# First layer of the sparse feed-forward with features on partitions, biases on 128 rows, six idle products a tile

## The reference

```python
# block 1: E=8 experts, F=1024, each token goes to one expert, weighted by its probability
h = jax.nn.gelu(x @ w1 + bb1, approximate=False)     # per expert, (tokens, F)
y = h @ w2 + bb2                                      # (tokens, 256)
# block 5: F=512, silu, each token goes to two experts, y = t + sum_k w_k * expert_k(t)
# block 7: F=256, gelu, each token goes to one expert, unweighted
```

## Time and profile before

| | |
|---|---|
| time, median of 3 runs (lowest, highest) | 2582.37 us (2580.01, 2584.39) |
| the profiled execution's own time | 2593.29 us |
| its span | 2591.3 us |
| mean granted clock of TensorE | 0.92 of full speed |
| PE busy / PEld busy | 2213.3 us (85%) / 1467.9 us (57%) |
| DVE / ACT / POOL busy | 1561.2 us (60%) / 1411.5 us (54%) / 953.2 us (37%) |
| tiles of block 1, from first to last product | about 319 to 483 us of the span |
| tiles of block 5 | about 1985 to 2135 us |
| tiles of block 7 | about 2496 to 2573 us |

### The profile page before, as it was taken

One profiled execution on the slowest core, in us unless ns is written; L12 is line 12 of the kernel. 1 busy time (PEld: TensorE's weight loads), 2 busy tenths in 40 slices (PEclk: granted clock), 3 DMA queues, 4 the chain that ended last, 5 costly groups with the idle time before them and its releaser, 6 DMA issues. The chain is left out here.

```text
span 2591.3 us, 62717 instructions
## 1 busy us (share of the span) xinstructions
PE 2213.3 (85%) x23986; PEld 1467.9 (57%) x23986; DVE 1561.2 (60%) x3640; ACT 1411.5 (54%) x2999; POOL 953.2 (37%) x1066
## 2 busy tenths in 40 slices
PE   5889399599999999968699999999974993899755
PEld 2556255367777777745456666666652541566533
DVE  3667572476566556636767777777756544556463
ACT  3666563365555555425466666666663542566543
POOL 3443222154444444404423333333322632433043
PEclk8999699799999999969899999999986995999978
DMA  6563361300000000010200000000023214333133
GB/s 129 111 116 71 111 216 38 119 20 14 14 14 8 14 14 2 2 33 1 87 14 9 15 14 9 15 14 9 2 85 103 67 56 124 87 79 73 26 114 109
DMA packets 118581, 139.59 MB, mean 54 GB/s; under 512 B 15072, under 2 KB 107184, under 8 KB 118288
## 3 DMA queue, kind: packets, MB, share of 16 engines
q1 hardware_dynamic: 110900, 115.39, 17.3%
q0 software_dynamic: 7392, 20.19, 2.5%
HBM read 93.25 MB, written 17.47 MB: 43 GB/s over the span
## 5 line engine op out<-in xcount | busy, mean ns | idle before, releaser
L952 DVE TENSOR_REDUCE a_mx<-a_pair 112x2 f32<-112x750 f32 x256 | 238.0, 936 | 194.9 <-PE a_pair L1021 194.9
L1260 POOL TENSOR_TENSOR a_kp<-a_kp 125x512 f16<-125x512 f32 x192 | 217.6, 1158 | 259.1 <-ACT a_kp L1351 259.1
L353 POOL TENSOR_SCALAR a_P<-a_P,a_inv 112x375 f32<-112x375 f32 x256 | 148.4, 593 | 378.5 <-DVE a_inv L484 377.4
L890 ACT ACTIVATE a_PT<-a_pair 125x672 f32<-125x672 f32 x256 | 186.2, 730 | 71.1 <-PE a_pair L1033 66.3
L391 ACT ACTIVATE a_P<-a_masked,a_least 112x375 f32<-112x375 f32 x256 | 153.5, 600 | 83.5 <-DVE a_least L479 81.6
L1394 DVE SCALAR_TENSOR_TENSOR a_k<-a_p,a_k 128x375 f16<-128x375 f32 x128 | 69.3, 547 | 138.7 <-ACT a_k L1307 138.7
L1351 ACT CAST a_kp<-a_kp 125x512 f16<-125x512 f32 x192 | 110.4, 617 | 76.4 <-DVE a_kp L1413 76.4
L572 PE MATMUL a_p<-a_kc,a_wk 128*128 128x375 f16 x768 | 147.1, 327 | 4.3 <-POOL a_kc L347 4.3
L1493 PE MATMUL a_p<-a_kc,a_wk 128*128 128x375 f16 x768 | 142.4, 327 | 6.3 <-POOL a_kc L1252 6.3
L586 PE MATMUL a_p<-a_wv,a_kc 128*125 128x512 f16 x576 | 141.9, 383 | 5.2 <-DVE a_v L518 3.6
L479 DVE CUSTOM_DVE_ANT_0 a_masked<-a_s,a_mask_add 112x375 f32<-112x375 f32 x256 | 129.9, 545 | 27.1 <-PE a_s L609 26.1
(11 more groups left out here) (446 smaller groups left out, 5324.1 us busy)
## 6 DMA issues: line engine op xcount, KB each, us to landing
a_kc<-in_ctxT SPq DMA_DIRECT2D x64, 375.0 KB, 4.0
a_k<-a_k_parts SPq DMA_DIRECT2D x192, 93.8 KB
w_stage<-in_L_ffn_W SPq DMA_DIRECT2D x32, 512.0 KB
w_stage<-in_L_ffn_ew SPq DMA_DIRECT2D x16, 512.0 KB, 6.9
w_stage<-expert_rows SPq DMA_DIRECT2D x16, 448.0 KB, 8.0
a_v_in_sb<-in_ctx SPq DMA_DIRECT2D x16, 375.0 KB
a_q<-a_q_parts SPq DMA_DIRECT2D x48, 112.0 KB, 3.6
w_stage<-in_L_ffn_W SPq DMA_DIRECT2D x16, 256.0 KB, 3.9
```

The costliest lines, as they stand in the source:

```text
L353: pool.tensor_scalar(P[:, p % 4, r, :], P[:, p % 4, r, :], inv[:, p % 4, r:r + 1], 1.0, ALU.mult, ALU.mult).then_inc(P_done, 1)
L890: act.activation(PT[:, p % 4, :, :], pair_bank[slot["turned", p]][0:KP, :, 0:KT * S], ACT.Exp).then_inc(exp_done, 1)
L952: dve.tensor_reduce(mx[:, b % 2, 2 * pair:2 * pair + 2], pair_bank[slot["score", p]][0:S, :, 0:SK], AX.X, ALU.max).then_inc(max_done, 1)
L1260: pool.tensor_tensor(kp16[:, LO, j, hf, r, :, :].rearrange("p c m -> p (c m)"), kp[:, n % 4, :], kp16[:, HI, j, hf, r, :, :].rearrange("p ...
```

## The change

hidden swaps the operands: a 128 x 128 piece of w1h is now stationary and x16 (128 columns) moves, so that features come out on partitions. For each 128 features there is one bias product and six products of 128 columns, in place of one and six of up to 512 columns for a whole block. The transposes of the hidden result, their copies and buffers (turn_parts, turn_h, take_high, take_low, hk, t_bank) go; ACT and DVE split the result in SBUF (high_h, low_h) for all three blocks. Block 1 runs output(j-1) in iteration j (LATE = 1), blocks 5 and 7 output(j-2) as before, with a third buffer for h16. There are four hidden banks (HR) for three. The bias operands rows, pick and ones16 are widened to 128 partitions, with zeros in the rows that are new; POOL clears rows during layernorm_phase. Block 7 has six idle products a tile.

```diff
-BUSY_START, BUSY_TILE = 48, 2
+BUSY_START, BUSY_TILE = 48, 6
-        self.pick = m.sb("pick", [2 * E, E, 128], F16)
+        self.pick = m.sb("pick", [128, E, 128], F16)
-        self.rows = m.sb("rows", [2, E, F + D] if self.flat else [2 * E, F + D], F16)
+        self.rows = m.sb("rows", [128, E, F + D] if self.flat else [128, F + D], F16)
+    def clear_rows(self, pool):
+        pool.memset(self.rows[:, :, :] if self.flat else self.rows[:, :], 0.0).then_inc(self.rows_clear, 1)
     def prepare_act(self, act):
         act.wait_ge(self.bias_in, 16)
+        act.wait_ge(self.rows_clear, 1)
-        layernorm_phase(nc, tag + "n", X, XT, ident, xn=xn, fetch=fetch)
+        layernorm_phase(nc, tag + "n", X, XT, ident, xn=xn, fetch=fetch, prepare=w.clear_rows)
-    HR, YR = 3, 3
+    HR, YR = 4, 3
+    LATE = 2 if early else 1
+    HB = LATE + 1
-        h16 = m.sb("h16", [128, 2, 2, F], F16)
+        h16 = m.sb("h16", [128, HB, 2, F], F16)
-        ident16, ones16, warm = m.sb("ident16", [128, 128], F16), m.sb("ones16", [2, 128], F16), m.sb("warm", [128, 1])
+        ident16, ones16, warm = m.sb("ident16", [128, 128], F16), m.sb("ones16", [128, 128], F16), m.sb("warm", [128, 1])
+                def turn_bias(out, e, cols):
+                    if w.flat:
+                        pe.matmul(out, w.rows[:, bass.ds(e, 1), cols].rearrange("z o f -> z (o f)"), ones16[:, :], start=True, stop=False)
+                    else:
+                        pe.matmul(out, w.rows[:, cols], r.pick[:, bass.ds(e, 1), :].rearrange("p o t -> p (o t)"), start=True,
+                                  stop=False)
...
                     for blk in range(NB):
...
-                        add_bias(bank[:, 0:BW], e, cols, start=True, stop=False)
-                        for i, (x, z) in enumerate(PARTS):
-                            for c in range(DC):
-                                mm = pe.matmul(bank[:, 0:BW], x16[:, j % 2, x, c, :],
-                                               w.w1h[:, z, c, bass.ds(e, 1), cols].rearrange("p o f -> p (o f)"),
-                                               start=False, stop=(i, c) == (2, DC - 1))
-                        mm.then_inc(h_done, 1)
                         for f in range(BW // 128):
                             at = blk * BW + f * 128
+                            out = bank[:, f * 128:(f + 1) * 128]
+                            turn_bias(out, e, slice(at, at + 128))
+                            for c in range(DC):
+                                for x, z in ((HI, HI), (LO, HI), (HI, LO)):
+                                    mm = pe.matmul(out, w.w1h[:, z, c, bass.ds(e, 1), at:at + 128].rearrange("p o f -> p (o f)"),
+                                                   x16[:, j % 2, x, c, :], start=False, stop=(c, z) == (DC - 1, LO))
+                        mm.then_inc(h_done, 1)
...
-                for j in range(NT + 2):
+                for j in range(NT + LATE):
...
-                    if 1 <= j < NT + 1:
-                        (turn_parts if early else turn_h)(j - 1)
-                    if j >= 2:
-                        output(j - 2)
+                    if j >= LATE:
+                        output(j - LATE)
...
                 def high_h(j):
-                    if j >= 2:
-                        act.wait_ge(o_done, j - 1)
+                    if j >= HB:
+                        act.wait_ge(o_done, j - HB + 1)
                     for blk in range(NB):
-                        n = j * NB + blk
-                        act.wait_ge(t_done, n + 1)
-                        act.copy(h16[:, j % 2, HI, blk * BW:(blk + 1) * BW], t_bank[n % 2][:, 0:BW]).then_inc(h_hi, 1)
+                        act.wait_ge(h_made, j * NB + blk + 1)
+                        act.copy(h16[:, j % HB, HI, blk * BW:(blk + 1) * BW],
+                                 hs[:, j % 2, blk * BW:(blk + 1) * BW]).then_inc(h_hi, 1)
```

More of the change, by code:

```diff
@@ L2027, in constants @@
                            pattern=[[1, S]], channel_multiplier=-1).then_inc(self.made, 1)
[L2028 removed]
+        pool.affine_select(out=self.pick[0:2 * E, :, :], in_=self.pick[0:2 * E, :, :], compare_op=ALU.not_equal, fill=1.0, base=0,
                            pattern=[[-1, E], [0, 128]], channel_multiplier=1).then_inc(self.blank, 1)
         pool.wait_ge(self.blank, 3)
[L2031 removed]
+        pool.affine_select(out=self.pick[0:2 * E, :, :], in_=self.pick[0:2 * E, :, :], compare_op=ALU.not_equal, fill=1.0, base=-E,
                            pattern=[[-1, E], [0, 128]], channel_multiplier=1).then_inc(self.made, 1)
@@ L2437, in hidden @@
-                        mm.then_inc(h_done, 1)
[L2439 to L2443, removed]
-                        for f in range(FC):
-                            mm = pe.transpose(t_bank[z][:, f * 128:(f + 1) * 128], hk[:, j % 2, z, f * 128:(f + 1) * 128],
-                                              ident16[:, :])
-                        mm.then_inc(t_done, 1)
@@ L2449, in turn_h @@
[L2449 to L2453, removed]
                         for f in range(BW // 128):
                             at = blk * BW + f * 128
-                            mm = pe.transpose(t_bank[(j * NB + blk) % 2][:, f * 128:(f + 1) * 128], hs[:, j % 2, at:at + 128],
-                                              ident[:, :])
-                        mm.then_inc(t_done, 1)
+                            out = bank[:, f * 128:(f + 1) * 128]
@@ L2704, in _ @@
                             w.make_low(dve, n)
-                    if early and j < NT:
-                        low_parts(j)
-                    if 1 <= j < NT + 1:
-                        (take_low if early else low_h)(j - 1)
-                    if j >= 2:
-                        add_y(j - 2)
+                    if j < NT:
+                        low_h(j)
+                    if j >= LATE:
+                        add_y(j - LATE)
                     if early:
```

59 lines of the change are left out of this document (17 added, 42 removed).

## The result

The changed kernel takes **2591.22 us** (median of 14 runs, 2584.16 to 2596.79), the kernel before 2583.80 (14 runs beside them, 2576.61 to 2591.27): a ratio of **1.003 [1.002, 1.0041]**, 7 us slower. 2562 was forecast, and 2591 lies outside the range of 2541 to 2589. The profiled execution took 2587.95 us, its span is 2586.2.

What follows compares the result with a forecast made beforehand. PE, or what feeds it, sets the pace; with the change TensorE's queue would. Block 1 -21, block 5 +4, block 7 -4 and the rest +0.5 sum to -20.5 us, a median of 2562 us, range 2541 to 2589.

Steps and rivals of the forecast that it cites:

- Products of 128 columns: First layer: 28 products of 128 columns start 0.055 us apart and cost 1.56 us, against 1.52 for seven wide ones.
- rival 2: Weight loads set the pace at 0.081 us each, block 1 takes 7.57 a tile; -6, 2576 us; chance 0.06.
- Biases on 128 rows: Widening removes 0.19 us lost around each narrow bias, three times a tile in block 1, twice elsewhere.
- Rival 4: The wide bias keeps its 0.19 us; block 1's engine sum is 7.7 a tile; about -3, 2579 us; chance 0.04.
- Addresses: TensorE's queue takes 0.124 us per run-time address; tiles of blocks 1, 5, 7 need 6.17, 4.19, 2.70 us.
- rival 3: Addresses cost more, losing from 138 ns; at 150 ns +18, 2600 us; or block 5's clock falls, +22; chance 0.15.
- Rival 1: Addresses are free, hidden behind products or merged; -52, 2530 us; chance 0.13.
- Block 1: After the first seven iterations tiles take 6.3 us, ending at 460 instead of 482.3; gain 21 us.
- keep doing so: Block 1's first seven iterations: ACT and DVE convert an expert in each, at about 7 us, unchanged.
- Block 5: First eight tiles stay at POOL's pace, 4.54; the other 27 take 4.19 for 4.01; loss 4 us.
- Block 7: 20 steps of 3.07 fall to 2.85 (floor 2.70), with a tail shorter by 0.5; gain 4 us.
- The rest: POOL's clearing of rows, 5.6 us at most, is covered in layer norm; +0 to 2 us, taken as 0.5.

Runs made afterwards that it cites:

- fix1: Changed kernel with the low parts of block 1's first-layer weights always from expert 0; 2590.86 us, 0.9967 of the kernel before.
- fixed57: Changed kernel with first layer and its bias in blocks 5 and 7 always from expert 0; 2563.74 us, 0.9876 of the kernel before.
- biasfix: Changed kernel with only the first layer's bias in blocks 5 and 7 always from expert 0; 2582.40 us, 0.9938 of the kernel before.
- pads: Kernel before with bias operands padded to 128 partitions in all three blocks, nothing else; 2567.16 us, 0.9889 of the kernel before.
- only5: Kernel before with the change in block 5 alone; 2594.38 us, 1.0045 of the kernel before.
- padstart: Kernel before with padded bias operands, plus 48 idle products ahead of block 5's first tile; 2570.50 us, 0.9892 of the kernel before.
- only1: Kernel before with the change in block 1 alone; 2574.04 us, 0.9964 of the kernel before.
- pad1: Kernel before with padded bias operands in block 1 only; 2589.20 us, 0.9959 of the kernel before.
- only7: Kernel before with the change in block 7 alone; 2586.36 us, 1.0018 of the kernel before.
- third job: Timing job on the second job's chip, with biasfix, pad1 and the changed kernel again (2597.18 us, 1.0000); the kernel before took 2597.33 us.
- first job: Timing job on one chip, with again, only1, only5 and only7; the kernel before took a median of 2582.49 us.
- again: The kernel before, unchanged, run for a second profile; 2583.93 us, 1.0001 of the kernel before.

## Why the prediction was wrong

The main mechanism was right: the queue of TensorE becomes the bound. Taking addresses away shows it in block 1 (fix1) and block 5 (fixed57, biasfix). In block 7 no run without addresses came out even; there the trace alone speaks for it, since 13 addresses at 0.132, 0.68 for the expert and 0.46 of waits make up the 2.86 without a rest. What failed were mainly four sizes: the price of an address, the old pace of block 7, the pace of block 5's first eight tiles, and an effect of block 1 on block 5 that the sum didn't have. Forecast -20.5, measured +7.4 us.

- **Products of 128 columns: right.** Starts 0.056 apart over 56 products. The rule of the Trainium skill ("TensorE: Matmul & The Clock Gate", section "Back-to-back issue gap"), some 81 ns per pair, is not what this trace shows; rival 2 is out. (By its price my engine sum of block 5 would have been 3.9, not the 4.0 that I wrote.)
- **Biases on 128 rows: right.** pads gives 0.62 us in a tile of block 1, where my price is 3 x 0.19 = 0.57. Rival 4 is out. But this gain doesn't need the rest of the change, which I didn't draw out. By my own price it is worth up to 0.57 x 21 + 0.38 x 56 = 33 us alone, more than the 20.5 of the whole forecast: by that estimate the other parts of the change cost time.
- **Addresses: the count right, the price too low.** I took 0.124 from one pair of loads. In ten tiles of block 5 of the changed kernel, 218 of 250 steps are at 0.124, and 32 take 0.19 on average: a mean of 0.1326. A tile then holds 25 x 0.1326 + 0.66 (expert) + 0.45 (waits) = 4.43, as measured. In block 1 the mean is 0.1327, and one more instruction of the queue, for the output's bias (L2419), takes 0.14: 41 x 0.1327 + 0.14 + 0.66 + 0.47 = 6.71, as measured. Some 0.0086 more for each of the 13 x 41 + 27 x 25 addresses on the path in blocks 1 and 5 is 10 of the 28 us between forecast and result. It is below rival 3's break-even of 0.138, so rival 3's price alone didn't decide. The lower clock that it named for block 5 is hardly seen: the granted clock is 1.00 from the ninth tile on, 2015 to 2126. Only among the first eight tiles it is 0.77 over 15 us (1997.3 to 2012.3), and they take 46.1 us there for 44.8 in only5, where it is 1.00 at that place. Rival 1 fell with biasfix.
- **Block 1: -21 forecast, -14 in the profiles.** Twelve steps at 6.71 instead of 6.3 are 5 us of the difference. The low parts of the last expert's first layer also start 2.0 us later, counted from the first tile (48.9 us for 46.9): "keep doing so", of ACT and DVE in the first seven iterations, was not quite so.
- **A term that no step had: block 1's gain is partly given back in block 5.** In all five profiles with block 1 as before, the first tile of block 5 comes 59.5 to 59.7 us after the start of its layer norm; in all other profiles but padstart's 61.6 to 62.3, over the same code. (It is not the clearing of rows: only1 doesn't clear them there and is late, only5 does and isn't.) The first eight tiles of block 5 take 40.6 to 40.9 us with the old form there and block 1 as before, and 42.7 in only1, but 40.7 in pad1. The windows of the first 30 us, only7 and then only1:

```profile
1912.90:1927.90 15.00, 8.80 (x35) 6.38 (x36) 11.28 (x50) 11.10 (x24) 0.00 (x0) 0.66 0.83 281
1927.90:1942.90 15.00, 13.07 (x46) 5.57 (x44) 2.21 (x3) 9.48 (x13) 8.57 (x14) 1.00 0.28 82
```
```profile
1909.40:1924.40 15.00, 8.72 (x34) 6.39 (x35) 11.24 (x50) 11.08 (x24) 0.00 (x0) 0.59 0.83 275
1924.40:1939.40 15.00, 14.28 (x36) 6.67 (x38) 1.94 (x2) 9.76 (x13) 8.57 (x14) 0.85 0.30 87
```

  PE does the same work at a granted clock of 0.85 instead of 1.00, and needs longer. All eighteen profiles show one of these two courses, 0.66 then 1.00 or 0.58 to 0.59 then 0.85. So of the -14 in the profiles 9.3 are left in only1's timed runs. What in block 1's stage decides the course was not tested. Whether the start of block 5 itself matters isn't known either: the lower course holds over starts from 1893.8 to 1910.9, the other over 1912.9 to 1924.0, so neither moves within 11 to 17 us, and only 2 us lie between the two groups.
- **Block 5: +4 forecast, +11.6 measured.** Two failures. The steps are 4.43, not 4.19, which is 6.5 us over 27 tiles. And "the first eight tiles go at POOL's pace, and stay" was wrong. POOL's timeline in the changed kernel (compare):

```profile
1997.74 1.72 POOL L2395 DMA_INDIRECT expert_rows<-f_y,f_dest  x1 [0.69 <-DVE f_y L2577]
...
2003.49 1.00 POOL L2395 DMA_INDIRECT expert_rows<-f_y,f_dest  x1 [2.04 <-DVE f_y L2577]
```

  POOL now waits for y, so it no longer sets their pace. These eight tiles take 44.8 us in only5 for 40.7; what sets them instead was not isolated. The end, with two sets of transposes less, is 2 to 3 us shorter where I took 1.
- **Block 7: -4 forecast, +4.6 measured.** The failed step is "20 steps of 3.07, against 2.49 in good stretches": my own rows held 2.49 as a tile without a gap, and I took the mean of one uneven execution for the pace. In the even execution the same twenty steps take 51.4 us, and in only7 58.8: 7.4 us more, less 2 at the two ends. My new pace of 2.85 came out at 2.86, partly by luck: the 0.15 above my floor of 2.70 was an allowance that I gave no source for, and it was in fact the dearer addresses (0.11) and the expert's reading (0.04). (Twenty steps from 3.07 to 2.85 and a tail of 0.5 are also 4.9 us and not the 4 that I put in.) Where the kernel before is uneven the loss isn't seen: in the third job the changed kernel is level with it (1.0000).
- **The rest: right as far as it can be seen.** Clearing rows costs nothing that the blocks' starts show: from the layer norm to the first tile block 1 takes 43.2 us in the changed kernel, 42.8 and 43.1 in the two profiles of the kernel before.

The sum by the runs: -14 + 4.5 (given back) + 11.6 + 4.6 = +7 us.

## What to carry to other kernels

Count what a change adds to the instruction queue of TensorE, one run-time address at a time, and take its mean over many, not the shortest pair: 0.133 us each here, for 0.124. Widening the rows of a narrow operand is worth trying alone: here it gave more than the reordering it came with, for some memory and one clearing. Before a stage's pace is taken from one profile, ask whether the profile's own time lies above the median: here it lay some 10 us above, and block 7, whose pace I read from it, was 8 to 12 us longer than in the first job's profiles of the same form.

## What the runs showed of the hardware

- In a stretch of short tiles ACT can start 1.87 us after the last product that it waits for has ended by its record, though it is idle. In the same stretch (the first profile of the kernel before, block 7) DVE starts 0.03 us after ACT has ended a y, nine times, and PE 0.06 after DVE, twice. Block 7 was uneven in all twelve profiles of the last three jobs, on two chips and in both forms, and in none of the first job's four. The kernel before took 2582 us there and 2595 to 2597 in the others. The uneven traces also lack about half of block 7's semaphore records (534 in the first profile's twenty steps, 950 in those of again); whether the recording has a part in it isn't known.
- Unchanged code ran 1.9 to 2.8 us longer, at a granted clock of 0.85 instead of 1.00 over 15 us, in every profile in which a block far ahead of it was 10 us or more shorter.
- An address that TensorE's queue works out at run time takes 0.124 us at least and 0.133 on average, reading an expert's number 0.66, a wait that doesn't have to wait 0.11.
- A bias product of 16 rows between products of 128 costs 0.2 us more around it than its columns (0.32 + 0.31 us to the next starts, for 0.22 + 0.21 with 128 rows, pads in block 1).
